# A two-layer graph network on one NeuronCore: new setup, regrouped window sums, the cross product on TensorE, wide spans tile by tile

## The reference, cut to what matters

```python
# layer 0
x1s, x1v = (s*a @ W + s*c @ W'), (v*a @ W + v*c @ W')        # l1; s_s, s_v in the same way (sc)
w0, w1, w2, w3 = split(silu(edge_attr_10 @ W_fc1) @ W_fc2)   # 10 -> 100 -> 192 = 64+64+32+32
gs, gv = x1s[src], x1v[src]
mid = [w0*gs*e_s, w3*(gv . e_v)/sqrt3, w1*gs*e_v (64x3), w2*gv*e_s (32x3)]
agg = segment_sum(mid, dst) / 4
m   = agg @ l2 (with attributes a and c);  o = m*mask @ l3
x   = layernorm(x + C_S*s_s + C_X*o_s, ...)
# layer 1
w1..w5 = split(silu(edge_attr_64 @ fc_w1 / 8) @ fc_w2 / 8)   # 64 -> 64 -> 224 = 64+64+32+32+32
es, ev = h_s[src], h_v[src]
mid_s = [w1*es*e0, w4*(ev . e1)/sqrt3]
mid_v = [w2*es*e1, w3*ev*e0, w5*cross(ev, e1)/sqrt2]
agg   = segment_sum(mid, dst) / 4
pre   = self projection + agg @ lin2
out   = layernorm(x + [silu(scalars), sigmoid(gates)*vectors])
```

## Time and profile before

| | us |
|---|---|
| three executions, median (lowest to highest) | 4457.3 (4451.7 to 4458.25) |
| the profiled execution's own time | 4453.04 |
| its span in the profile | 4451.0 |
| setup, to the first gather | 0 to 138.0 |
| edge stage of layer 0, first to last gather | 138.0 to 2098.1 |
| nodes of layer 0, to the first gather of layer 1 | to 2338.4 |
| edge stage of layer 1, first to last gather | 2338.4 to 4298.6 |
| last groups and nodes of layer 1 | to 4451.0 |
| busy: PE, PEld, DVE, ACT, POOL | 4044.4, 3053.2, 2847.8, 2961.5, 3054.0 |
| busy share of the span, in the same order | 91%, 69%, 64%, 67%, 69% |

### The profile page before, as it was taken

How to read it: one execution, slowest core, us unless ns; L and a number is a source line. 1 busy time by engine, 2 the same in 40 slices (tenths; PEclk the granted TensorE clock), 3 DMA queues, 4 the chain that set the end, 5 groups by cost and what they waited for, 6 DMA issues and landing times. The chain is left out here.

```text
span 4451.0 us, 166762 instructions
## 1 busy us (share of the span) xinstructions
PE 4044.4 (91%) x58000; PEld 3053.2 (69%) x58001; DVE 2847.8 (64%) x7746; ACT 2961.5 (67%) x12216; POOL 3054.0 (69%) x3215
## 2 busy tenths in 40 slices
PE   7888888888888888888979999999999999999987
PEld 4677777777777777776756766666666666666666
DVE  4544444444444444444667888888888888888878
ACT  1566666666666666665337877777777777777753
POOL 2577777777777777776017777777777777777751
PEclk9999999999999999999889999999999999999995
DMA  4222222222222222223334444444444444444433
GB/s 107 71 72 73 72 72 72 72 73 73 72 73 73 72 72 72 72 73 68 104 98 129 121 120 120 122 121 120 121 121 121 121 121 121 122 121 121 121 100 94
DMA packets 356348, 430.11 MB, mean 97 GB/s; under 512 B 203298, under 2 KB 248648, under 8 KB 356112
## 3 DMA queue, kind: packets, MB, share of 16 engines
q0 software_dynamic: 156288, 329.79, 27.4%
q1 hardware_dynamic: 199618, 98.11, 8.2%
q10 hardware_dynamic: 400, 1.68, 0.1%
HBM read 405.56 MB, written 23.74 MB: 96 GB/s over the span
## 5 line engine op out<-in xcount | busy, mean ns | idle before, releaser
L415 POOL DMA_INDIRECT e_rows<-scratch_table,e_index x3136 | 2967.3, 946 | 1010.5 <-issue 926.2
L438 ACT ACTIVATE e_match<-e_match,e_attr 128x40 f32<-128x40 f32 x10976 | 2480.9, 315 | 176.3 <-DMA e_attr<-in_edge_attr 172.1
L470 PEld LDWEIGHTS e_sum<-e_match,e_msg 128*64 128x64 f32 (+1 forms) x50176 | 1714.0, 125 | 698.3 <-DVE e_msg L629 244.3
L470 PE MATMUL e_sum<-e_match,e_msg 128*64 128x40 f32 (+2 forms) x50176 | 1846.2, 223 | 247.5 <-DVE e_msg L626 194.6
L461 PE MATMUL e_w<-k_fc,e_hidden 100*128 100x192 f32 (+1 forms) x4704 | 1275.2, 407 | 0.0
L618 DVE TENSOR_TENSOR e_msg<-e_w,e_rows 128x512 f32<-128x512 f32 x784 | 537.8, 686 | 1008.1 <-DMA e_rows<-scratch_table,e_index 980.0
L461 PEld LDWEIGHTS e_w<-k_fc,e_hidden 100*128 100x128 f32 (+1 forms) x4704 | 833.0, 190 | 385.3 <-issue 364.8
L431 ACT ACTIVATE e_hidden<-e_h 100x512 f32<-100x512 f32 (+1 forms) x784 | 384.4, 490 | 925.9 <-PE e_h L450 921.2
L450 PE MATMUL e_h<-e_inputs,k_fc 128*100 128x512 f32 (+1 forms) x1568 | 708.6, 534 | 57.9 <-DMA e_inputs<-in_inputs 27.0
L608 DVE TENSOR_TENSOR e_misc<-e_misc,e_rows 128x384 f32<-128x384 f32 x392 | 221.8, 566 | 354.2 <-DMA e_rows<-scratch_table,e_index 354.1
L624 DVE TENSOR_TENSOR e_msg<-e_w,e_rows 128x384 f32<-128x384 f32 x784 | 428.1, 546 | 0.0
(11 more groups left out here) (122 smaller groups left out, 1454.0 us busy)
## 6 DMA issues: line engine op xcount, KB each, us to landing
e_rows<-scratch_table,e_index POOLq DMA_INDIRECT x3136
e_inputs<-in_inputs SPq DMA_DIRECT2D x196, 256.0 KB
e_attr<-in_edge_attr SPq DMA_DIRECT2D x392, 24.0 KB, 1.7
e_inputs<-in_inputs SPq DMA_DIRECT2D x196, 40.0 KB
e_index<-in_src SPq DMA_DIRECT2D x392, 4.0 KB
scratch_self<-m_h SPq DMA_DIRECT2D x10, 480.0 KB, 4.5
f_self<-scratch_self POOLq DMA_DIRECT2D x10, 480.0 KB, 5.0
m_xrow<-in_x POOLq DMA_DIRECT2D x10, 400.0 KB, 5.0
```

The source lines that it names most:

```text
L415: pool.indirect_dma_start(out=rows[j][:, t, :], out_offset=None, in_=table_dram, in_offset=bass.IndirectOffsetOnAxis(ap=index[q][:, c:c + ...
L438: last = nc.scalar.activation(match[j][:, t, c, :], match[j][:, t, 4, :], ACT.Copy, scale=attr[q][:, e0 + t, e:e + 1])
L470: return nc.tensor.matmul(out[rows, c0:c0 + n, :], m[:, t, f:f + rows.stop - rows.start], m5[:, t, which:which + n, :], start=(first and t ...
```

## The change

**Setup.** Rewritten. Inputs of all tiles stay resident and are loaded first, by SyncE, in five chunks of 2, 4, 8, 16 and 20 tiles; the projections need only two weight tensors. Six result banks instead of two. Columns of the table's rows are in the order scalars, vectors, so that one store goes out where two did, in 11 pieces. The clear of the sums is eight pieces. VectorE's work on destinations stands between tiles; the running sum is three short additions and one product on TensorE with a triangular matrix; the table goes through DRAM to one partition. The weights' scalings go to ScalarE, between tiles from the 24th on. The fold of `l2` and `l3` is four products after tile 38. Indices of the first groups and the relative destinations are kept tensors, loaded or made in the setup; the first gathers wait for nothing.

**Edge stages.** Gathered rows have 160 columns in both layers. The layout of the sums is new, with four chunks in both layers. A tile has two 64-wide products on the lower 64 columns of the array (120 and 40 moving columns) and 32-wide ones of 40 columns that alternate between the third and the fourth quarter of its columns: six in layer 0, twelve in layer 1. In layer 1 `fc2_1` is 128 x 256, with the weights in either half of its rows and a block of -w5 behind w5; each tile's weights are a product of its own on 64 rows of the array, lower and upper half in turn. VectorE writes w5 and -w5 times the gathered vectors, and the products by e1's components in `narrow_sums` make the cross product of them in the sums. The path for wide spans goes tile by tile, with buffers of one tile. The warm-up products have 256 columns.

**Nodes of layer 0.** The sums have four chunks, all copied and all cleared. The aggregated products are three of 96 rows by 64 columns and one of 128 by 128 with a smaller `out0` (128 x 192). `table1` has 160 columns and one store fewer. The first indices of the next stage are loaded here.

**Nodes of layer 1.** The four products have 32, 32, 32 and 96 columns, with a smaller `out1` (128 x 160).

```diff
@@ setup_phase @@
+        CHUNKS = (0, 2, 6, 14, 30, NT)
+        STORES = (0, 5, 10, 15, 20, 25, 30, 35, 40, 45, 48, NT)
+        UNIT, RING = 5, 4
+        PIECES = 8
...
-            nc.gpsimd.memset(sums[:, :, :], 0.0)
+            for c in range(PIECES):
+                nc.gpsimd.memset(sums[:, :, c * step:(c + 1) * step], 0.0)
...
+            def part(n):
+                act.wait_ge(node_mm, n + 1)
+                at_least(act, h_ready, n - 3)
+                nc.scalar.activation(part_a[n % 4][:, :], ps_node[n % 6][:, 0:D], ACT.Copy,
+                                     scale=w["attr"][:, n, 0:1]).then_inc(part_ready, 1)
...
-            pe.wait_ge(l_in, 32)
-            for c in range(16):
...
-            pe.wait_ge(weights_in, 16 * len(DIRECT))
+            pe.wait_ge(node_in, 32)
+            def project(n):
+                if n in CHUNKS:
+                    pe.wait_ge(x_in[CHUNKS.index(n)], 32)
+                at_least(pe, h_ready, n - 5)
+                cols = slice(n * P, (n + 1) * P)
+                out = ps_node[n % 6][:, 0:2 * D].rearrange("p (a n) -> p a n", a=2)
+                nc.tensor.matmul(out[:, :, S:D], x_v[:, cols], w["node_v0"][:, 0:192], start=True, stop=True)
+                nc.tensor.matmul(out[:, :, 0:S], x_s[:, cols], w["node_s0"][:, 0:128], start=True,
+                                 stop=True).then_inc(node_mm, 1)
...
+            for n in range(NT):
+                project(n)
+                if n == 28:
+                    count_extras()
+                if n == 38:
+                    fold_out0()
...
+            for n in range(NT):
+                add_c(n)
+                if n == 11:
+                    lowest()
+                if n == 15:
+                    highest()
+                if n == 17:
+                    spans()
+                if n == 20:
+                    totals()
+                if n in (22, 24, 26):
+                    partial((n - 22) // 2)
+                if n == 33:
+                    table_entries()
+                if n == 37:
+                    relative()
@@ edge_phase @@
-            sp.dma_start(dst_rel[:, 0:T], d["dst_rel"]).then_inc(dst_in, 16)
...
-                pool.wait_ge(prepared, 1)
-                pool.wait_ge(index_in[q], count)
-                pool.wait_ge(msg_done[j], count)
+                if not isinstance(count, int):
+                    pool.wait_ge(prepared, 1)
+                    pool.wait_ge(index_in[q], count)
+                    pool.wait_ge(msg_done[j], count)
...
+                fc2, n = w[f"fc2_{L}"], layer.wn
                 for u in range(TPG // layer.tiles_per_product):
-                    c0, n = u * layer.tiles_per_product * WPITCH, w[f"fc2_{L}"].shape[1]
-                    last = nc.tensor.matmul(ps_w[j % 2][:, c0:c0 + n], hidden[j % 2][:, u * P:(u + 1) * P], w[f"fc2_{L}"][:, :],
-                                            start=True, stop=True)
+                    for h in range(layer.tiles_per_product):
+                        c0, k = (u + 2 * h) * WPITCH, fc2.shape[0] // layer.tiles_per_product
+                        last = nc.tensor.matmul(ps_w[j % 2][:, c0:c0 + n], hidden[j % 2][k * h:k * h + k, u * P:(u + 1) * P],
+                                                fc2[k * h:k * h + k, :], start=True, stop=True)
...
+            def wide_sums(out, m, m5, opens, closes):
+                product(out, slice(0, 64), 0, m, 64, m5, 0, n=3, start=opens)
+                product(out, slice(0, 64), 3, m, 0, m5, 3, stop=closes)
+            def narrow_sums(out, m, m5, opens, closes):
+                low, high = slice(64, 96), slice(96, 128)
+                product(out, low, 0, m, 128, m5, 3, start=opens)
+                product(out, high, 3, m, 224, m5, 0, start=opens)
+                product(out, low, 1, m, 160, m5, 3)
+                if L == 0:
+                    product(out, high, 3, m, 256, m5, 1)
+                    product(out, low, 2, m, 192, m5, 3, stop=closes)
+                    return product(out, high, 3, m, 288, m5, 2, stop=closes)
+                product(out, high, 0, m, 352, m5, 2)
+                product(out, low, 2, m, 320, m5, 1)
+                product(out, high, 0, m, 480, m5, 1)
+                product(out, low, 2, m, 448, m5, 0)
+                product(out, high, 1, m, 384, m5, 0)
+                product(out, low, 3, m, 256, m5, 1)
+                product(out, high, 1, m, 416, m5, 2)
+                product(out, low, 3, m, 288, m5, 2, stop=closes)
+                return product(out, high, 2, m, 192, m5, 3, stop=closes)
...
-                nc.tensor.matmul(ps_h[:, 0:480], w["ident"][:, :], w["out1"][:, :], start=True, stop=True)
+                nc.tensor.matmul(ps_h[:, 0:256], w["ident"][:, :], w["fc2_1"][:, :], start=True, stop=True)
...
-                    nc.vector.tensor_tensor(comps(cross_a), e3(3), comps(r[:, :, 96:192]), ALU.mult)
-                    nc.vector.tensor_tensor(comps(cross_b[:, :, :]), e3(2), comps(r[:, :, 128:224]), ALU.mult).then_inc(crossed, 1)
...
-                    nc.vector.tensor_tensor(m[:, :, 320:416], cross_a, cross_b[:, :, :], ALU.subtract).then_inc(subtracted, 1)
...
-                    last = nc.vector.tensor_tensor(comps(m[:, :, 320:416]), w_v(192), comps(m[:, :, 320:416]), ALU.mult)
+                    nc.vector.tensor_tensor(comps(m[:, :, 320:416]), w_v(192), comps(r[:, :, 64:160]), ALU.mult)
+                    last = nc.vector.tensor_tensor(comps(m[:, :, 416:512]), w_v(224), comps(r[:, :, 64:160]), ALU.mult)
@@ layer0_nodes_phase @@
-            nc.gpsimd.memset(sums[:, 0:3, :], 0.0)
+            nc.gpsimd.memset(sums[:, :, :], 0.0)
...
-                sp.dma_start(rows("table1")[:, :, D:D + 2 * V], h1[s][:, :, 0:2 * V]).then_inc(stored[s], 16)
...
-                nc.tensor.matmul(agg, staged[b][:, 1, :], w["out0"][:, 0:320], start=True, stop=False)
-                nc.tensor.matmul(agg[:, :, 0:64], staged[b][:, 0, :], w["out0"][:, 320:448], start=False, stop=False)
-                nc.tensor.matmul(agg[:, :, 64:160], staged[b][:, 2, :], w["out0"][:, 448:640], start=False,
-                                 stop=True).then_inc(out_mm, 1)
+                for c in range(3):
+                    nc.tensor.matmul(agg[:, :, V * c:V * c + V], staged[b][0:MID, c, :], w["out0"][0:MID, 0:2 * V], start=True, stop=True)
+                nc.tensor.matmul(agg[:, :, V3:D], staged[b][:, 3, :], w["out0"][:, 2 * V:192], start=True, stop=True).then_inc(out_mm, 1)
@@ layer1_nodes_phase @@
+                for c in range(3):
+                    at = V if c == 2 else 0
+                    nc.tensor.matmul(o[:, V * c:V * c + V], staged[b][:, c, :], w["out1"][:, at:at + V], start=True, stop=True)
+                nc.tensor.matmul(o[:, V3:O1], staged[b][:, 3, :], w["out1"][:, 2 * V:2 * V + S1], start=True, stop=True).then_inc(out_mm, 1)
```

476 lines of the change are left out of this document (230 added, 246 removed).

## The result

The changed kernel takes 4522.39 us, median of four runs (4521.77 to 4524.62); the kernel before 4457.77 beside it. The ratio is 1.0149, 95% interval 1.0131 to 1.0167: slower by 1.5%, clear of the noise, as forecast (4509, range 4450 to 4590), by 65 us where 52 were forecast.

The account below looks back on a forecast made before the run. The prediction took GpSimd's gathers to bound both edge stages, with TensorE close behind in the second, and TensorE with its clock to bound the rest. Sum: 4453 - 42 + 1 + 91 + 10 - 4 = 4509 us, range 4450 to 4590.

Parts of the forecast that it names:

- Setup: Waits and steps around the projections removed, projections still 1.66 us each: first gather at 96 instead of 138.0 us, -42.
- the first is smaller, so they start at about 5: Setup: the first input block is under 240 KB, which lands in 3.2 us, so projections start at about 5 us.
- Edges of layer 0: First edge stage: TensorE grows from 4.44 to 4.76 us a group, hidden under the gathers' 5.00; +1 us.
- Nodes of layer 0: Layer 0's node stage: shorter tiles but half clock throughout, plus longer ends; together +91 us.
- 0.50 throughout: Layer 0's node stage: TensorE's clock stays at half rate, 5.73 us a tile, +81.8 us over 48 intervals.
- the turns at 0.50, the clear and the early index: Ends of layer 0's node stage: pipeline's last turns +5.8, memset of the sums +5.4, early index load saves 2 us.
- Edges of layer 1: Second edge stage: TensorE's group reaches 5.00 us, the gathers' own pace, and can't catch up early losses; +10 us.
- My base of 4.80: Second edge stage: TensorE's 4.80 us a group before the change, to which -0.54, -0.12 and +0.86 were added.
- Last stage: Layer 1's nodes: TensorE's 2.34 us a tile shorten by some 0.2 for 32 tiles, others lose full clock; -4 us.
- Rival (b): Layer 1's edges: the row halves don't overlap, +337 us, total 4846; half overlapped 4680; chance 0.06.
- Rival (c): Setup and node stage: back-to-back products are enough for the full clock, total 4368 us; chance 0.04.
- Rival (a): Layer 0's node stage: the clock rises as before, stage -11 us, total 4409, faster; chance 0.10.

Follow-up runs that it names:

- e1: Changed kernel with the scalars' product of layer 0's node stage widened back to 320 columns (192 zeros); node stage 364.4 us.
- e3: Kernel before with the 320-column product of layer 0's node stage cut into five of 64 columns; node stage 262.4 us.
- e4: Changed kernel with every 64-row product of setup and layer 0's node stage given 96 rows, the added ones zero; node stage 285.5 us.
- e7: e4 with all products of layer 0's node stage except the transposes on 128 rows, the added ones zero; node stage 236.8 us.
- e5: Changed kernel with layer 1's per-edge weights back as one product of 128 rows and 512 columns for two tiles; 4769.7 us.
- e8: e7 with the clear of the sums in pieces of five tiles between GpSimd's loads; 4371.75 us, ratio 0.9803 to the kernel before.
- e10: e8 with VectorE's and ScalarE's waits for stores split in layer 0's node stage; node stage 226.6 us.
- e2: Kernel before with the 320-column product of layer 0's node stage cut into two of 160 columns; node stage 254.4 us.

## Why the prediction was right

**Setup**, -42 forecast, -37.9 measured. The tiles are 1.66 us apart and the 192-column passes take 606 ns, as forecast. The four us are at the start: the first projection at 6.8 us instead of 5, and 4.1 us behind the second tile, waiting for the second chunk of inputs, a wait that my step "the first is smaller, so they start at about 5" did not look at:

```profile
PE s_psn L256 <- DMA s_xs<-in_xT_s: 4.1, 1, 4.1
```

The five small products cost 2.1 us for the 2.5, and the end is 1.4 shorter.

**Edges of layer 0**, +1 against -1.1. TensorE is busy for 0.33 us a group more (383.6 us for 357.2 in the 400 us from 1000), as forecast, and the gathers hide it.

**Nodes of layer 0**, +91 against +87.0. The forecast that decided the sign, 0.50 throughout, held. A tile took 5.83 us and not 5.73: the aggregated passes 1.86 for 1.77. The reason given for the clock was wrong, though. I wrote that the change takes just the longest passes away. Back in place they did not raise it (e1), and without them it rose (e3). What the change took away, next to columns, is rows: aggregated products on 96 instead of 128. That this alone would do was not tried in the kernel before; what e4 and e7 show is that the same passes on all rows rise where those on 96 do not. I also saw the gap between 96- and 64-row products in the rows as part of a tile's price and not as something to be removed; it was 1.1 us of the 5.83. The ends of the stage were the term put too high: the tiles came to +84.0 for +81.8, but what lies before and behind them to +3.0, where the turns at 0.50, the clear and the early index made 9.2. The clear grew by 5.4 us as forecast; VectorE stood behind it for 19.3 us and not the 21 of the forecast, 3.4 more than before.

**Edges of layer 1**, +10 against +17.6. Three terms held: hidden layer and weights -0.55 for -0.54, the 64-wide phase 1.26 for 1.28, the 32-wide one 1.71 for 0.86 + 0.86. Between turns of the loop a group takes 4.946 us, a hair under the gathers' 5.00. The term missing was the turn: 0.40 us more at it than between other groups, where the kernel before had 0.2; over four groups that makes 5.045 a group, and 392 x 0.045 = 17.6. My base of 4.80 had the old turn in it, and I carried it over unchanged. What makes the turn longer was not tried.

**Last stage**, -4 against +4.1. The step that failed is taking TensorE as its bound. At 0.50 the median distance between tiles is 2.307 us in both kernels, although TensorE's share fell from 70.5 of 75.0 us to 62.1 of 74.5. A chain through ScalarE and VectorE sets it, as the waits for `f_staged` and `f_pre` suggest; which step of it was not tried. Nor did "others lose the full clock" cost much: from the third tile to the last the kernel before needs 105.4 us, the changed one 106.1. Most of the 4 us lie ahead of the first tile. The last addition to the sums comes 16.3 us behind the last gather, where it came 13.2 behind it (before, then after; the last gathers start at 4298.6 and 4364.2):

```profile
4311.78 0.32 DVE L557 TENSOR_TENSOR sums<-sums,e_sum 128x160 f32 x1 [4.13 <-PE e_sum L470]
```

```profile
4380.45 0.32 DVE L607 TENSOR_TENSOR sums<-sums,e_sum 128x160 f32 x1 [3.40 <-PE e_sum L503]
```

The last messages wait for TensorE's weights there; that TensorE, now as slow as the gathers, is further behind when they end is my reading of it. The sum had no term for that.

Rival (b) fell by e5. Rival (c) fell by the node stage's 233 busy us at 0.50. Rival (a) named about the right price for a clock that rises: its node stage was 11 us under that of the kernel before, and e7's, less the 10 us of later start, is 227, 13 under it; but e7 also has no steps to 64 rows, so the two are not the same kernel.

## What to carry to other kernels

Read a product's rows as well as its columns: in this kernel, zero rows that make it 96 or 128 removed a fifth of a node tile's time on TensorE and a third of a setup tile's, because no step to 64 rows is left. They brought the full clock in parts of the setup with 96 rows, and back in the node stage only with 128. With that and one clear moved (e8) the changed kernel is 3.3% faster than as it was and 2.0% faster than the kernel before. When two engines are within 1% of each other, count the turn of the loop too. And look what runs on GpSimd beside a VectorE step before splitting a wait: e10's split gave nothing, since the clear held VectorE in the same tiles.

## What the runs showed of the hardware that I had not expected

- TensorE, busy in each of 233 us, stayed at 0.50 (the changed kernel), and so it did in e4 at 4.69 us a tile; e4's passes on 128 rows were at 1.00 within 10 us of the first tile (e7), and at 0.89 on average in the tiles. What else has a part in it stays open: the setup of e4 rose on 96 rows.
- In the runs beside which the kernel before takes 7525 us, TensorE stands in the edge stages between two passes and waits for nothing the profile shows: 3295 times before the sums' products in e7, half of these under 0.5 us, the longest 3.3. These products (busy, mean ns of one, idle before them and what ended it):

```profile
L503 PE MATMUL e_sum<-e_match,e_msg 128*32 128x40 f32 (+2 forms) x68992 | 3344.2, 226 | 2082.8 <-issue 2063.7
```

  In e2, which issues 78 passes a group in layer 1 instead of 122, the second edge stage took 3624 us, in e7 4273. The same chip showed the kernel before at 4461.29 us (beside e8) and at 7525.63 (beside e10), so it isn't the chip, and no run tells what it is; that the instructions come late is my reading of "issue". The kernel with fewer and longer passes lost less there.
- The clear by GpSimd and VectorE's scaling of a tile (L875, L884) don't run side by side: the scaling ends with the clear, at 2.25 us as at 21.6.
